# Probabilities times v in an attention loop: three split products per block replaced by one full fp32 product, with v read straight from two tiles

## The reference, cut to what matters

```python
q = (hidden_states @ Wq.T) ...            # 32 heads of 128
k = (cross_attention_states @ Wk.T) ...   # 8 heads of 128, each used by 4 query heads
v = (cross_attention_states @ Wv.T) ...   # the same
q = _rmsnorm(q, q_norm_w); k = _rmsnorm(k, k_norm_w)
scores = jnp.einsum('bhqd,bhkd->bhqk', q, k) * scale + attention_mask
probs = jax.nn.softmax(scores, axis=-1)
out = jnp.einsum('bhqk,bhkd->bhqd', probs, v)     # the product that is changed
return out.transpose(0, 2, 1, 3).reshape(bsz, q_len, H * HD) @ Wo.T
```

## Time and profile before

| | |
|---|---|
| runs before | 1420.07 us, median of 3 (1419.88 to 1420.27) |
| profiled execution, its own time | 1419.22 us |
| its span in the trace | 1417.5 us |
| PE busy | 1404.9 us (99% of the span) |
| DVE, ACT, POOL busy | 849.7 (60%), 514.4 (36%), 358.8 us (25%) |
| chain of work that ended last | PE 80%, DVE 2%, DMA 1% of the span |

### The profile page before, as it was taken

How to read it: one execution, slowest core, us unless ns; L and a number is a source line. 1 busy time by engine, 2 the same in 40 slices (tenths; PEclk the granted TensorE clock), 3 DMA queues, 4 the chain that set the end, 5 groups by cost and what they waited for, 6 DMA issues and landing times.

```text
span 1417.5 us, 26787 instructions
## 1 busy us (share of the span) xinstructions
PE 1404.9 (99%) x9135; PEld 1125.2 (79%) x9136; DVE 849.7 (60%) x1807; ACT 514.4 (36%) x1117; POOL 358.8 (25%) x374
## 2 busy tenths in 40 slices
PE   8999999999999999999999999999999999999998
PEld 7888887878787878787877878787878888777777
DVE  6444446656666666666666666666678746244458
ACT  5333344333333334333433343333334331222242
POOL 1122123121212121212121212111112101367746
PEclk9999999999999999999999999999999999999999
DMA  6544431111111111111111111111123344555548
GB/s 214 188 126 141 126 111 47 31 42 33 47 32 39 38 41 38 35 37 42 38 34 39 42 37 34 39 41 38 48 73 102 97 149 148 195 192 170 169 149 298
DMA packets 91229, 125.46 MB, mean 89 GB/s; under 512 B 7184, under 2 KB 57360, under 8 KB 90896
## 3 DMA queue, kind: packets, MB, share of 16 engines
q1 hardware_dynamic: 83632, 99.70, 22.2%
q0 software_dynamic: 7520, 24.65, 5.2%
HBM read 86.84 MB, written 37.49 MB: 88 GB/s over the span
## 4 chain that ended last, share of the span: by engine, by line
PE 80%; DVE 2%; DMA 1%; issue 1%; ACT 0%; POOL 0%; DVEq 0%; SPq 0%; ACTq 0%
PE ps L592 19%; PE ps L594 18%; PE ps L593 18%; PE ps L978 5%; PE ps L679 5%; PE ps L721 4%; PE ps L994 3%; PE ps L687 2%; PE ps L706 2%; PE ps L973 1%; DVE acc L1877 1%; DVE acc L1884 1%; DMA ybuf<-ye,didx 1%; PE ps L891 1%; DMA y<-ybuf 0%
## 5 line engine op out<-in xcount | busy, mean ns | idle before, releaser
L489 POOL CAST vth<-vt 128x256 fp32r<-128x256 f32 x64 | 25.4, 397 | 629.6 <-PE ps L721 627.6
L1482 DVE TENSOR_TENSOR al<-ps,ah 128x256 fp32r<-128x256 f32 x256 | 95.9, 416 | 116.4 <-ACT ah L1164 116.4
L1164 ACT CAST ah<-ps 128x256 fp32r<-128x256 f32 x256 | 83.5, 383 | 194.8 <-PE ps L594 188.3
L1476 DVE TENSOR_TENSOR acc<-ps,acc 128x512 f32 (+1 forms) x128 | 87.9, 687 | 109.0 <-PE ps L594 109.0
L592 PE MATMUL ps<-hT,w0h 128*128 128x512 f32 (+1 forms) x384 | 152.2, 396 | 0.0
L594 PE MATMUL ps<-hT,w0h 128*128 128x512 f32 (+1 forms) x384 | 149.9, 390 | 0.0
L593 PE MATMUL ps<-hT,w0l 128*128 128x512 f32 (+1 forms) x384 | 149.5, 389 | 0.0
L483 POOL TENSOR_TENSOR qr<-qv,mhalf 128x8 f32<-128x8 f32 x64 | 105.1, 1642 | 83.2 <-DVE qv L1491 83.2
L1133 ACT COPY qs<-ps 128x512 f32<-128x512 f32 x128 | 75.3, 588 | 120.8 <-PE ps L594 120.8
L1142 ACT ACTIVATE pb<-pb 128x256 f32<-128x256 f32 x128 | 48.3, 418 | 166.1 <-DVE pb L1509 166.0
L592 PE MATMUL ps<-w0l,ah 128*128 128x512 f32 x256 | 102.9, 402 | 0.0
(11 more groups left out here) (238 smaller groups left out, 3077.9 us busy)
## 6 DMA issues: line engine op xcount, KB each, us to landing
wraw<-in_w_att SPq DMA_DIRECT2D x64, 256.0 KB, 2.6
vbuf<-vo SPq DMA_DIRECT2D x16, 512.0 KB, 3.3
kbuf<-ko SPq DMA_DIRECT2D x16, 512.0 KB, 3.8
kt<-kbuf SPq DMA_DIRECT2D x32, 256.0 KB, 2.9
vt<-vbuf SPq DMA_DIRECT2D x64, 128.0 KB, 2.1
wgu<-in_w_gu SPq DMA_DIRECT2D x4, 2048.0 KB, 8.5
y<-ybuf SPq DMA_DIRECT2D x16, 512.0 KB, 6.8
xt<-in_x SPq DMA_DIRECT2D x16, 256.0 KB, 4.0
```

What stands on the lines that cost most here:

```text
L1164: act.copy(ah[:, bp, :, b2, :], pv_view(bp, b2)).then_inc(a_hi, 1)
L1476: dve.tensor_tensor(dst, PS[6 + bp][:], dst, ALU.add).then_inc(acc_done, 1)
L1482: dve.tensor_tensor(al[:, bp, :, b2, :], pv_view(bp, b2), ah[:, bp, :, b2, :], ALU.subtract).then_inc(a_lo, 1)
```

## The change

The three split matmuls of each block and half become one full float32 matmul. So the transposed probabilities are kept as float32 in one tile `pt`, with one eviction by ACT (`probs_out`) and none by DVE. v isn't split: PE reads it from the tiles into which SP loads it, `vt0` in even and `vt1` in odd steps, each with its own semaphore. SP reloads a tile as soon as the `probs_v` that read it last is done. A tile of 1280 words that nothing uses keeps the other tiles at their places. DVE's scaling of the scores, which overwrites `pb`, gets an explicit wait for the transposes of the step before, since the subtraction that implied it is gone.

```diff
-            v_hi = sb("vth", [P, 2, HD], F32R, a)
+            vt_odd = sb("vt1", [P, 2, HD], F32, a)
...
-            vt = sb("vt", [P, 2, HD], F32, a)
-            vhl = [v_hi, sb("vtl", [P, 2, HD], F32R, a)]
-            pt = [sb(f"pt{'hl'[q]}", [P, 4, HG * S], F32R, a) for q in range(2)]
+            vt = [sb("vt0", [P, 2, HD], F32, a), vt_odd]
+            pt = sb("pt", [P, 4, HG * S], F32, a)
+            sb("staged_values", [P, 1280], F32, a)
...
+            def load_v(i, q):
+                sp.dma_start(vt[q][:].rearrange("p b t -> p (b t)"), vbuf[i]).then_inc(vt_in[q], 16)
...
-                sp.wait_ge(v_split, 2 * i + 2)
-                sp.dma_start(vt[:].rearrange("p b t -> p (b t)"), vbuf[i + 1]).then_inc(vt_in, 16)
+                sp.wait_ge(pv_done, 2 * i + 2)
+                load_v(i + 1, 1 - odd)
...
-            def split_v(j):
-                pool.wait_ge(vt_in, 16 * j + 16)
-                pool.wait_ge(pv_done, 2 * j + 2)
-                pool.sem_inc(pool_mark, 1)
-                pool.tensor_copy(vhl[0][:], vt[:]).then_inc(v_split, 1)
-                pool.wait_ge(v_split, 2 * j + 1)
-                pool.tensor_tensor(vhl[1][:], vt[:], vhl[0][:], ALU.subtract).then_inc(v_split, 1)
...
             def probs_v(r, part):
-                pe.wait_ge(v_split, 2 * r + 2)
+                pe.wait_ge(vt_in[part], 8 * (r - part) + 16)
                 pe.wait_ge(a_hi, 4 * r + 4)
                 pe.wait_ge(a_lo, 4 * r + 4)
                 for bp in range(2):
                     if part == 0:
-                        pe.wait_ge(pT_hi, 2 * r + 3 + bp)
                         pe.wait_ge(pT_evac, 2 * r + 3 + bp)
-
-                    for z, (v_part, p_part) in enumerate(((0, 1), (1, 0), (0, 0))):
-                        for b2 in range(2):
-                            rows = slice(b2 * S, (b2 + 1) * S)
-                            mm = pe.matmul(PS[4 + b2][:, bp * 256:(bp + 1) * 256], vhl[v_part][rows, bp, :],
-                                           pt[p_part][rows, 2 * part + bp, :], start=(z == 0), stop=(z == 2))
-                            if bp == 1 and z == 2:
-                                mm.then_inc(pv_done, 1)
+                    for b2 in range(2):
+                        rows = slice(b2 * S, (b2 + 1) * S)
+                        mm = pe.matmul(PS[4 + b2][:, bp * 256:(bp + 1) * 256], vt[part][rows, bp, :],
+                                       pt[rows, 2 * part + bp, :], start=True, stop=True)
+                        if bp == 1:
+                            mm.then_inc(pv_done, 1)
...
-            def probs_hi(i, odd, bank=2):
+            def probs_out(i, odd, bank=2):
                 act.wait_ge(pT_done, i + 1)
                 if odd:
                     for q in range(2):
-                        act.copy(pt_odd(0, q), pT_odd(q, bank)).then_inc(pT_hi, 1)
+                        act.copy(pt_odd(q), pT_odd(q, bank)).then_inc(pT_evac, 1)
                 else:
                     act.wait_ge(pv_done, 2 * i + 2)
-                    act.copy(pt_even(0), pT_even()).then_inc(pT_hi, 2)
+                    act.copy(pt_even(), pT_even()).then_inc(pT_evac, 2)
...
                 dve.wait_ge(s_done, j + 1)
+                if not isinstance(j, int) or j > 0:
+                    dve.wait_ge(pT_done, j)
                 dve.tensor_tensor(pb[:], PS[3][:].rearrange("p (b s) -> p b s", s=S), per_row(qr),
                                   ALU.mult).then_inc(s_scaled, 1)
...
-            def probs_lo(i, odd, bank=2):
-                if odd:
-                    for q in range(2):
-                        dve.wait_ge(pT_hi, 2 * i + 1 + q)
-                        dve.tensor_tensor(pt_odd(1, q), pT_odd(q, bank), pt_odd(0, q), ALU.subtract).then_inc(pT_evac, 1)
-                else:
-                    dve.wait_ge(pT_hi, 2 * i + 2)
-                    dve.tensor_tensor(pt_even(1), pT_even(), pt_even(0), ALU.subtract).then_inc(pT_evac, 2)
```

More of the change, by code:

```diff
@@ L238, in build @@
         w0_in, w_hi, w_lo, acc_zero = sem("w0_in"), sem("w_hi"), sem("w_lo"), sem("acc_zero")
-        wr_in, kt_in, vt_in = sem("wr_in"), sem("kt_in"), sem("vt_in")
+        wr_in, kt_in, vt_in = sem("wr_in"), sem("kt_in"), [sem("vt_in0"), sem("vt_in1")]
         q_done, q_copy, q_sq, ss_done, q_var, q_rt = (
@@ L244, in build @@
             sem("s_sum"), sem("s_rcp"), sem("p_ready"))
-        ss_turned, v_split, pT_hi = sem("ss_turned"), sem("v_split"), sem("pT_hi")
+        ss_turned = sem("ss_turned")
         pT_done, pT_evac, pv_done, a_hi, a_lo, o_done, acc_done = (
@@ L337, in _ @@
                     sp.wait_ge(v_stored, 16 * 2 + 16)
-                    sp.dma_start(vt[:].rearrange("p b t -> p (b t)"), vbuf[0]).then_inc(vt_in, 16)
+                    load_v(0, 0)
                 if n == 1:
@@ L483, in inverse_root @@
                 pool.tensor_tensor(qr[:], qv[:], mhalf[:, 0:8], ALU.pow).then_inc(q_rt, 1)
-            def split_v(j):
-                pool.wait_ge(vt_in, 16 * j + 16)
-                pool.wait_ge(pv_done, 2 * j + 2)
-                pool.sem_inc(pool_mark, 1)
-                pool.tensor_copy(vhl[0][:], vt[:]).then_inc(v_split, 1)
-                pool.wait_ge(v_split, 2 * j + 1)
-                pool.tensor_tensor(vhl[1][:], vt[:], vhl[0][:], ALU.subtract).then_inc(v_split, 1)
             inverse_root(0)
-            split_v(0)
             pool.wait_ge(w_hi, 8)
@@ L504, in _ @@
             inverse_root(2)
-            split_v(1)
-            split_v(2)
             with pool.Fori(3, STEPS - 2) as j:
                 inverse_root(j)
-                split_v(j)
             root_of_variance(0)
@@ L570, in pT_odd, with pt_odd, pt_even @@
             return PS[bank + q][:, 0:2 * P].rearrange("p (m n) -> p m n", m=2)
-        def pt_odd(x_, q):
-            return pt[x_][:].rearrange("p (m q) n -> p m q n", q=2)[:, :, q, P:2 * P]
+        def pt_odd(q):
+            return pt[:].rearrange("p (m q) n -> p m q n", q=2)[:, :, q, P:2 * P]
         def pT_even():
             return PS[6][:].rearrange("p (m n) -> p m n", m=4)
-        def pt_even(x_):
-            return pt[x_][:, :, 0:P]
+        def pt_even():
+            return pt[:, :, 0:P]
         def act_part(c, it, x_):
@@ L1176, in act_step @@
                 if odd:
-                    probs_hi(i, 1)
+                    probs_out(i, 1)
                 q_out(1, i + 1)
@@ L1181, in act_step @@
                 if not odd:
-                    probs_hi(i, 0)
+                    probs_out(i, 0)
                 a_hi_tile(i - 1, 1)
@@ L1197, in _ @@
             squares(1, 1)
-            probs_hi(0, 0)
+            probs_out(0, 0)
             split_slice(0, W[1], 0)
@@ L1205, in _ @@
             squares(1, 2)
-            probs_hi(1, 1, 6)
+            probs_out(1, 1, 6)
             split_slice(1, W[1], 1)
@@ L1216, in _ @@
             a_hi_tile(1, 0)
-            probs_hi(2, 0)
+            probs_out(2, 0)
             a_hi_tile(1, 1)
@@ L1286, in _ @@
             split_slice(i + 1, W[0], NC - 1)
-            probs_hi(i + 1, 1)
+            probs_out(i + 1, 1)
             a_hi_tile(i, 0)
@@ L1546, in dve_step @@
                 i = 2 * d + odd
-                if odd:
-                    probs_lo(i, 1)
                 if complete[0] is not None:
@@ L1555, in while_root @@
                 def while_root():
-                    if not odd:
-                        probs_lo(i, 0)
                     add_out(2 * i - 1, 1, tile_before)
@@ L1571, in opening @@
             def opening():
-                softmax(1, lambda: probs_lo(0, 0), lambda: None)
+                softmax(1)
                 slice_lo(0, W[1], 0)
-                softmax(2, lambda: probs_lo(1, 1, 6), lambda: a_rest(0, 0))
+                softmax(2, lambda: None, lambda: a_rest(0, 0))
                 a_rest(0, 1)
```

## The result

| | before | after |
|---|---|---|
| median | 1420.17 us (1419.88 to 1421.35, 4 runs) | 1433.16 us (1432.90 to 1434.08, 4 runs) |
| profiled execution, its span | 1417.5 us | 1431.4 us |

The ratio is 1.0085, with a 95% interval of 1.0072 to 1.0097: slower. A later comparison with more rounds (e6) gives 1432.99 against 1421.32 us, a ratio of 1.0084 (1.0070 to 1.0098), so the loss is about 12 us. The forecast was 1430.1 in a range of 1428 to 1445; the range held, and the measured time lies 3 us over the likeliest value.

The account below looks back on a forecast made before the run. PE was taken to bound the loop, so only its product counted: 1419.22 us profiled, plus 10.2 for 64 steps, less 0.2 coming back, plus 0.85 to the runs' median, gave 1430.1 us, in a range of 1428 to 1445.

Parts of the forecast that it names:

- What bounds the kernel: Attention loop: PE, busy in every microsecond from 260 to 1000 us; work taken from DVE, ACT or POOL gains nothing.
- The price of the product: PE's product: four float32 turns (start-to-start distances) of 0.216 us replace six of 0.1175; 0.159 us a step, 10.2 us slower.
- The edges: Product's first and last distances: 0.11 and 0.09 us dearer than a plain pair, unchanged; 0.33 and 0.31 us after.
- The sum: Whole kernel: 1419.22 + 10.2 − 0.2 = 1429.2 us, with 0.85 back for the median of the runs, 1430.1 us.
- what may come back: PE's waits at the loop's ends: the longer product takes in the 0.4 us wait for DVE; 0.2 us for both.
- The staircase: Product's passes in strict call order: five turns instead of four, 13.8 us more, 1443.9 us; chance 0.12.
- The open weight load: Product: every pass's weight load in the open, three more turns cost 0.11; 21 us more, 1451; chance 0.04.
- serial halves: Product: row halves in full float32 don't run side by side, eight turns; 55 us more, 1485; chance 0.04.
- The hidden case: Product beside a wait of PE: the 0.16 us goes into the wait and nothing is measured; chance 0.02.
- The rival on the other side: Product: a pass on half the rows takes one beat a column, four turns of 0.1175; 15.0 us less, 1405; chance 0.03.

Follow-up runs that it names:

- e6: Changed kernel, unchanged, measured with more rounds: 1432.99 us against 1421.32 for the kernel before, ratio 1.0084.
- e2: Changed kernel with its product put back to twelve fp32r calls, three times the same one, everything else of the change kept: 1420.60 us against 1421.27, ratio 0.9994.
- e3: Changed kernel with each full float32 call issued twice, eight calls a step instead of four: 1485.23 us, ratio 1.0455 to the kernel before.
- e4: Changed kernel with the product of the upper half of the rows left out, two calls a step: 1431.49 us against 1421.27 before, ratio 1.0073.
- e1: Kernel before with only PE's part of the change, four full float32 calls on the high parts, casts and splits kept: 1432.90 us against 1421.27, ratio 1.0079.
- e7: Changed kernel with the same four calls reordered, both blocks of the lower row half first, then the upper: 1432.15 us, ratio 1.0077 to before.
- e9: Changed kernel with one fp32r call for each full float32 call, products with low parts left out: 1417.12 us against 1422.10 before, ratio 0.9953.
- e10: Kernel before without the product of v's low part, eight fp32r calls a step: 1416.80 us against 1422.10, ratio 0.9958.
- e11: The one-fp32r-product kernel (e9) with three output projection matmuls moved from behind the scores to ahead of the product: 1390.04 us against 1421.68 before, ratio 0.9777.
- e12: Complete kernel before with the same three output projection matmuls moved ahead of the product: 1424.76 us against 1421.68, ratio 1.0022.

## Why the prediction was right, and where it was off

**What bounds the kernel: right.** PE is busy throughout the loop before and after, and e2 shows that all the work taken off DVE and POOL is worth 0 (ratio 0.9994).

**The price of the product: right.** A turn of full float32 was put at 0.216 us from the experts' product, with both row halves in it, from the column parts of `q_sums`. The product's share of the step grew from 0.91 to 1.06 us by the timelines; over all 64 steps the records give sums of 58.3 and 68.4 us, so 10.1 us or 0.158 a step, against 10.2 and 0.159 in the prediction. (Two profiles of the changed kernel and three of the one before agree on both sums within 0.02 us.) e3 confirms the turn with 0.87 for four, e4 that the second half is free.

**The edges: right.** The first distance and the last were carried over from the fp32r product, at 0.33 and 0.31 us, and 1.06 came out for 1.07; the records have 0.32, twice 0.216, and 0.31.

**The sum: 3 us under the measured 1433.2.** The product's own term fits within 0.1 us, and three other things make the rest. First, the split products: from the first scores to the last the loop grew by 10.8 us (mean of profiles), and the 62 products in it account for 9.8. The other 1.0 us lies in the split products, mostly in the first ten behind the new product, a few nanoseconds on each. The prediction had no term for it. It shows in every profile with four full float32 calls in a step, or two (the changed kernel's two, e1, e4, e7), but not in e3 with eight, and its cause stays open. Second, the expert stage, which the change doesn't touch: it was 146.3 us in the profile on which the sum was made and 150.0 in the first of the changed kernel. It doesn't follow the product. With full float32 products it takes 146.6 (e3) to 150.0 us, and with split or single fp32r products alone 146.3 to 150.1 (e9; e10 has 149.8). Third, the baseline: 1420.07 for the runs shown, 1421.3 to 1422.1 in the later comparisons, and in the comparison with most runs of the changed kernel the difference is 11.7 us. So one of the 3 us is the split products, and the rest is the baseline and the expert stage, by chance as far as is known. The sum's term for what may come back, 0.2 us, is below all this, but it came as said: the wait for DVE went from 0.4 to 0.2.

**Rivals.** The staircase (0.12) is excluded by 1.06 us, and e7 excludes it even in an order that ought to have brought it out. The open weight load and the serial halves fall with the same 1.06 and with e3 and e4. The hidden case falls with the whole. The rival on the other side, a turn of one beat a column with 15 us gained, was wrong in its turn, and also in its consequence: it took for granted that a shorter product shortens the step. e9 and e10 show that in most steps it doesn't. Of the 0.47 us that e9's product is shorter, most steps lose 0.08, and all steps together 7.3 us of 30. The prediction read "PE waits for nobody" as "anything saved on PE counts in full", and the profile had the row against it: ACT's copy ends 0.21 us ahead of the scores (707.31 and 707.52), and in e9 they start 0.12 us behind its end, so only the rest could be won. The forecast of a loss didn't need that row. One of a gain would have failed by it.

## What to carry to other kernels

Replacing three split products by one full float32 product was no saving here, where the matrix engine is the bound: it was two passes of 0.216 us in place of three of 0.1175, although it took a third of the calls and freed two other engines. Price such a change by distances between starts, of the same type and width, found anywhere in the trace. Where an engine is busy in the whole of a stretch, work added to it counts in full, but work taken away counts only down to the next thing that it covers; so, before promising a gain, look for the operand of the next instruction and when its producer ends. When the cover is the limit, move other ready work of the same form in front of it (e11: 5 us became 32).

## What the runs showed of the hardware beyond what was expected

- The two row halves of the array worked through full float32 passes independently of each other: with the order of the program half by half, eight passes still took four turns (1.07 us), and leaving a half out saved nothing (1.06).
- A pass of 256 columns on half the rows costs 0.216 us in full float32, the same as on all 128 rows in the experts' product, and about 0.1175 in fp32r, with two calls in a block (e10) as with three. Other widths weren't tried on half the rows.
- The expert stage, with its indirect transfers, varies from 146.3 to 147.8 us with the same code, and from 146.3 to 150.1 over all the profiles of this study. A single profile per kernel can't resolve 2 us in this program.
- Moving three matmuls of the complete kernel to another place in each step, with no wait before or after, cost 3 us (e12). Of these 1.4 are in the loop, which remains unexplained, and the rest in the expert stage, which the move doesn't touch.
